# Attention weights of a graph layer as the larger of two exponentials instead of a bent row, a GpSimd addition and one exponential

## The chip, the cores and the metric

One core of a Trainium2 chip. The metric is the time of one execution on the device in microseconds, the median of several runs.

## The reference

Four layers of a graph network over 625 nodes with 256 features and 20000 edges. The change is in layer 1, an attention layer with 4 heads of 64 features:

```python
h = (x @ W).reshape(n, H, F)
a_src = jnp.sum(h * att_src[None], axis=-1)
a_dst = jnp.sum(h * att_dst[None], axis=-1)
e = jax.nn.leaky_relu(a_src[src] + a_dst[dst], 0.2)
m = jax.ops.segment_max(e, dst, num_segments=n)
ex = jnp.exp(e - m[dst])
denom = jax.ops.segment_sum(ex, dst, num_segments=n)
alpha = ex / (denom[dst] + 1e-16)
out = jax.ops.segment_sum(h[src] * alpha[..., None], dst, num_segments=n)
```

The output is 625 x 256 numbers in float32. Layers 0, 2 and 3 and the norms between them are not touched.

## The kernel before, in words

The edges are turned into a dense matrix of counts (`adjT`, sources on the partitions, destinations along the row), in 5 tiles of 125 nodes. Layer 1 then works densely: for each head `h` (4) and each tile `s` of 125 sources (5), so for 20 items `i = 5h + s`, it makes a tile of 125 sources by 625 destinations of attention weights, multiplies it by the counts, and adds its product with the features to that head's sums. All waits between engines are written out by hand with semaphores; each engine runs its own list in order.

- TensorE spreads a column of 625 numbers as a row over all partitions (`spread_row`, five products with the identity). ScalarE copies each spread row out of PSUM (`copy_row`, L520 is its helper). Eight rows stand ahead of the items: `src_row` for 4 heads and `dst_row` for 4 heads.
- VectorE, `best(h, b)`, L1008: the maximum over a destination's sources, one operation for a head and a tile; `down_of(h)`, L1017 to L1021, makes from it the column that brings the row's maximum to zero (`down`). Heads 0 and 1 are done ahead of the items, heads 2 and 3 between them (`AHEAD = 2`). TensorE spreads `down` as one more row per head (`spread_down`), ScalarE copies it over `src_row[h]`.
- An item: ScalarE's `bend`, L629, a Relu of `dst_row` with a bias; GpSimd's addition of `src_row`, L466; ScalarE's `exp`, L636; VectorE's `weigh`, L1027 (`min` with 1, times `adjT`); TensorE's product, the mix, two column ranges into PSUM (it counts up `mixed`). `score` has 7 slots, which a `bend` takes again when the mix of 7 items earlier is done.
- After a head: ScalarE copies its sums (`copy_sums`), TensorE turns them (`turn_sums`, L1406), and VectorE divides and adds the bias (`take_sums`, L1034 to L1043).

ScalarE's list of the stage before:

```python
new_row = {0: 0, 2: 1, 10: 2, 15: 3}
for i in range(HEADS + 2):
    if i < HEADS:
        bend(i)
        if i in new_row:
            copy_row(2 * H + new_row[i])
    if i >= 2:
        exp(i - 2)
    if i >= NT + 3 and i % NT == 3:
        copy_sums(i // NT - 1)
```

Behind the stage come two norms, and then layer 2, whose GpSimd gathers (84 pairs) take the larger part of the kernel; they wait for a table that is stored after these norms.

## Time and profile before

| | us |
|---|---|
| median of 3 runs | 508.77 |
| the runs | 508.77, 507.05, 510.25 |
| the profiled execution, its own time | 509.2 |
| its span | 507.4 |
| busy: TensorE / VectorE / ScalarE / GpSimd | 391.4 / 308.2 / 193.9 / 277.6 |
| the stage of the change: first spread row to the last head's sums | 124.30 to 190.49 |

The busy times are sums over the whole span. The profile names engines PE (TensorE), PEld (TensorE's weight loads), DVE (VectorE), ACT (ScalarE) and POOL (GpSimd). Tiles that share a buffer appear under the buffer's name: `score` is `q_sb`, `arena` or `x`, and `src_row`, `dst_row` and `adjT` are `arena`. PEclk is the granted clock of TensorE as a share of 2.4 GHz.

### The profile page before, as it was taken

Reading aid. Unit: us, or ns where it says so; the run is one execution under the profiler, and the core shown is the slowest. Engines: PE = TensorE matmul, PEld = TensorE weight load, DVE = VectorE, ACT = ScalarE, POOL = GpSimd, SP = SyncE. Lnnn points to the kernel's source line nnn. Section 1 sums busy time; section 2 is a strip of 40 time slices with the busy share of each in tenths; the row PEclk is TensorE's granted clock in tenths of the full one; section 3 lists DMA queues with packets and bytes.
Section 4 is the critical chain, followed back from the end, with each engine's and each line's share of the span. In section 5 each row is a group of like instructions: output and inputs, shape, how many; then the busy total and the mean of one; then the engine's idle time right before and its main releaser. Section 6 shows DMA issues by size and latency. Waiting matters only on the chain.

```text
span 507.4 us, 5439 instructions
## 1 busy us (share of the span) xinstructions
PE 391.4 (77%) x1414; PEld 210.4 (41%) x1415; DVE 308.2 (61%) x596; ACT 193.9 (38%) x497; POOL 277.6 (55%) x278
## 2 busy tenths in 40 slices
PE   2936675799757865897999995799999989889800
PEld 0612222476714432433554542454544444347700
DVE  3479999777699979444444541454455854445243
ACT  1623997314676550253333332243333323212310
POOL 5274875004594540017777777777777777744120
PEclk9878799999857697797999998799999999999965
DMA  5921122000000000036777776777777777720001
GB/s 152 199 83 47 47 70 54 1 1 0 2 1 0 0 1 0 26 105 199 211 210 211 208 213 179 219 209 212 209 210 206 200 213 208 208 59 1 2 3 53
DMA packets 24231, 56.20 MB, mean 111 GB/s; under 512 B 5964, under 2 KB 11279, under 8 KB 24198
## 3 DMA queue, kind: packets, MB, share of 16 engines
q0 software_dynamic: 16224, 48.06, 33.9%
q1 hardware_dynamic: 6800, 6.58, 5.3%
q10 hardware_dynamic: 1174, 1.16, 0.8%
q8 instruction: 16, 0.26, 0.2%
q14 instruction: 17, 0.14, 0.1%
HBM read 53.37 MB, written 2.40 MB: 110 GB/s over the span
## 4 chain that ended last, share of the span: by engine, by line
PE 41%; DVE 19%; POOL 15%; DMA 12%; issue 7%; ACT 4%; ACTq 0%; POOLq 0%; DVEq 0%
PE ps L1198 37%; POOL arena L472 11%; DMA arena<-q_table,t_odd 5%; DVE arena L852 5%; DVE q_sb L1027 3%; DMA hot_table<-x 2%; DMA w_lr<-in_L_gnn_W_r 2%; DVE x L1008 2%; DMA arena<-hot_table,t_even 1%; DVE arena L847 1%; DVE arena L1107 1%; POOL adj L472 1%; DVE stats L920 1%; PE ps L1342 1%; POOL al_g L502 1%
## 5 line engine op out<-in xcount | busy, mean ns | idle before, releaser
L1107 DVE TENSOR_TENSOR arena<-arena,ps 128x1024 f32<-128x1024 f32 x84 | 102.6, 1221 | 111.9 <-DMA arena<-q_table,t_odd 96.1
L1198 PE MATMUL ps<-arena,hot 128*128 128x512 f32 x336 | 165.1, 615 | 0.5 <-DVE arena L1107 0.5
L472 POOL DMA_INDIRECT arena<-q_table,t_even x84 | 79.5, 947 | 68.3 <-DMA q_table<-q_sb 43.1
L472 POOL DMA_INDIRECT arena<-q_table,t_odd x84 | 80.8, 962 | 25.6 <-issue 25.6
L1198 PE MATMUL ps<-parts,hotT 125*128 x168 | 77.5, 543 | 17.1 <-DVE arena L1107 14.2
L1198 PEld LDWEIGHTS ps<-arena,hot 128*128 128x128 f32 x336 | 58.5, 194 | 50.8 <-issue 43.4
L520 ACT ACTIVATE hotT<-ps 125x128 fp32r<-125x128 f32 x84 | 23.3, 277 | 145.9 <-PE ps L1455 145.9
L1198 PEld LDWEIGHTS ps<-parts,hotT 125*128 125x128 f32 x168 | 30.7, 195 | 65.7 <-issue 65.4
L1198 PE MATMUL ps<-arena 128*128 128x376 f16 (+1 forms) x178 | 34.8, 345 | 21.4 <-DVE arena L852 10.8
L852 DVE TENSOR_SCALAR arena<-iota,t_column,t_weight 128x376 f16<-128x376 f16 x140 | 45.3, 396 | 0.0
L434 POOL DMA_INDIRECT arena<-hot_table,t_even x28 | 30.6, 1093 | 13.7 <-issue 6.7
L680 ACT ACTIVATE hot<-h_sb,ones 128x128 fp32r<-128x128 f32 x84 | 32.8, 392 | 0.0
L672 ACT ACTIVATE h_sb<-iota,t_dst 128x128 f32<-128x128 f32 x84 | 32.5, 389 | 0.0
L1198 PE MATMUL ps<-q_sb,h_ones 125*65 125x512 f32 (+1 forms) x48 | 21.8, 596 | 13.8 <-DVE q_sb L1027 13.8
L1198 PEld LDWEIGHTS ps<-arena 128*128 128x128 f16 x178 | 14.8, 104 | 41.3 <-issue 38.2
L466 POOL TENSOR_TENSOR q_sb<-q_sb,arena 125x625 f32<-125x625 f32 x12 | 19.2, 1621 | 18.3 <-ACT q_sb L629 11.5
L563 ACT ACTIVATE x<-iota,t_dst 128x128 f16<-128x128 f16 x84 | 25.9, 388 | 8.1 <-issue 4.8
L1198 PE MATMUL ps<-zeros 128*128 128x512 f16 (+1 forms) x70 | 19.2, 427 | 8.9 <-POOL ident L396 4.2
L1027 DVE SCALAR_TENSOR_TENSOR q_sb<-q_sb,arena 125x625 f32<-125x625 f32 x12 | 19.9, 1674 | 5.8 <-ACT q_sb L636 5.8
L1008 DVE CUSTOM_DVE_ANT_0 x<-arena 125x625 f32<-125x625 f32 x20 | 21.4, 1103 | 2.0 <-ACT arena L520 2.0
L520 ACT ACTIVATE arena<-ps 125x625 f32<-125x625 f32 (+3 forms) x20 | 12.6, 637 | 22.6 <-PE ps L1505 14.9
L520 ACT ACTIVATE xT<-ps 128x500 f32<-128x500 f32 (+2 forms) x13 | 6.9, 553 | 36.6 <-PE ps L1198 18.7
(231 smaller groups left out, 539.0 us busy)
## 6 DMA issues: line engine op xcount, KB each, us to landing
arena<-q_table,t_even POOLq DMA_INDIRECT x84, 3.7
arena<-q_table,t_odd POOLq DMA_INDIRECT x84, 3.7
q_table<-q_sb SPq DMA_DIRECT2D x5, 250.0 KB
w_sb<-in_L_gnn_W SPq DMA_DIRECT2D x1, 1024.0 KB, 12.9
x<-in_x ACTq DMA_DIRECT2D x1, 625.0 KB
out<-x SPq DMA_DIRECT2D x5, 125.0 KB
w_sb<-in_L_gnn_W SPq DMA_DIRECT2D x1, 512.0 KB, 12.2
hot_table<-x SPq DMA_DIRECT2D x1, 459.0 KB
```

The lines of the kernel that those rows point to most:

```text
L434: pool.indirect_dma_start(hot_src[:, j, k, 0, :], None, hot_dram[:, :], bass.IndirectOffsetOnAxis(ap=t_even[:, at:at + 1], axis=0)).then_i ...
L466: nc.gpsimd.tensor_tensor(w, w, src_row[0:NP, h, :], ALU.add).then_inc(leaky, 1)
L472: pool.indirect_dma_start(to, None, q_dram[:, :], bass.IndirectOffsetOnAxis(ap=index, axis=0)).then_inc(done, 16)
L520: return nc.scalar.activation(o, i, ACT.Copy)
L563: last = nc.scalar.activation(apart[:, j, k, :], iota16[:, 0:128], ACT.Abs, bias=t_dst[:, two_item(g, k, 1)], scale=-1.0)
L672: nc.scalar.activation(off_by[:, i % 3, :], iota32[:, :], ACT.Abs, bias=t_dst[:, 2 * i:2 * i + 1], scale=-1.0).then_inc(off_by_done, 1)
L680: nc.scalar.activation(hot[:, i % U, :], off_by[:, i % 3, :], ACT.Relu, bias=ones[:, 0:1], scale=-1.0).then_inc(hot_built, 1)
L852: last = V.tensor_scalar(hot_src[:, j, k, r, :], iota16[:, 0:SHARED], t_column[:, at], t_weight[:, at], ALU.is_equal, ALU.mult)
L1008: step(V.tensor_tensor_reduce(out=spare[len(last_steps) % len(spare)], in0=mask[0:NP, b, 0:N], in1=src_row[0:NP, h, :], scale=1.0, scalar= ...
L1027: V.scalar_tensor_tensor(score[i % SLOTS], score[i % SLOTS], 1.0, adjT[0:NP, s * N:(s + 1) * N], ALU.min, ALU.mult).then_inc(weighted, 1)
L1107: V.tensor_tensor(both, both, ps[:, 5 + i % 2, :].unsqueeze(1).to_broadcast([128, 2, HID]), ALU.max).then_inc(maxed, 1)
L1198: return nc.tensor.matmul(o, a, b, start=start, stop=stop, skip_group_check=True)
```

## The change

With z = a_src + a_dst and m the row's maximum after the leaky relu, exp(max(z, 0.2z) - m) is the larger of exp(z - m) and exp(0.2z - m). Each is one ScalarE pass: an Exp over a spread row with the source's term as bias. So there are two spread rows for each head (`down` = a_dst - m, `down_flat` = 0.2 a_dst - m), both made by `down_of`, and the four rows of `a_dst` are not spread any more. ScalarE's two passes per item are `exp_above` and `exp_below`; VectorE takes the larger of the two in an operation of its own (`join`), one item ahead of `weigh`. The addition on GpSimd and the tile `src4` are gone. `score` is split in 4 slots (`above`, taken again when the mix of 4 items earlier is done) and 3 (`below_zero`, taken again after the join of 3 items earlier). ScalarE copies a head's two rows after the third item of the head before. The two new rows use PSUM where the second bank of turned sums was, so `turn_sums` now has one bank and waits for the sums before to be read.

```diff
@@ -191,6 +191,7 @@
         a3 = a2 + H * N
         top = sb("top", [128, NT, H], f32)
         down = sb("down", [128, NT, H], f32)
+        down_flat = sb("down_flat", [128, NT, H], f32)
         rden = sb("rden", [128, NT, H], f32)
         p0 = U * 2 * HID
         ring = arena[:, 0:p0].rearrange("p (i r f) -> p i r f", i=U, r=2)
@@ -208,13 +209,14 @@
         q_flat = q_sb[:, :, :].rearrange("p b f -> p (b f)")
         score = [q_flat[0:NP, k * N:(k + 1) * N] for k in range(4)] + [arena[0:NP, a3:a3 + N]]
         score += [x0[:, :, :].rearrange("p b f -> p (b f)")[0:NP, k * N:(k + 1) * N] for k in range(2)]
-        SLOTS = len(score)
+        MET = 4
+        above, below_zero = score[0:MET], score[MET:]
+        FLAT_SLOTS = len(below_zero)
 
         prod = [q_sb[:, n, :].rearrange("p (c f) -> p c f", c=DC) for n in range(4)]
         h_ones = sb("h_ones", [128, NT, H, F + 1], f32)
 
         xl, xr = h_ones[:, :, :, :].rearrange("p b h f -> p b (h f)")[:, :, 0:D + 1], x1_bias
-        src4 = sb("src4", [128, NT, H], f32)
         src02 = sb("src02", [128, NT, H], f32)
         hot = sb("hot", [128, U, 128], f32r)
         hotT = sb("hotT", [128, 2, 128], f32r)
@@ -264,7 +266,7 @@
         agg_done, var_ready, std_ready, x_ready = sem("agg_done"), sem("var_ready"), sem("std_ready"), sem("x_ready")
         h_done, h_copied, row_done, row_copied = sem("h_done"), sem("h_copied"), sem("row_done"), sem("row_copied")
         src_scaled, down_ready = sem("src_scaled"), sem("down_ready")
-        bent, leaky, exped, weighted, mixed = sem("bent"), sem("leaky"), sem("exped"), sem("weighted"), sem("mixed")
+        exped, joined, weighted, mixed = sem("exped"), sem("joined"), sem("weighted"), sem("mixed")
         bias_added = sem("bias_added")
         sumT_copied, sum_turned, sum_read = sem("sumT_copied"), sem("sum_turned"), sem("sum_read")
         q_done, q_copied, q_stored = sem("q_done"), sem("q_copied"), sem("q_stored")
@@ -288,7 +290,7 @@
 
         def row_bank(r):
 
-            return 1024 * (r % H) if r < 2 * H else NT * 512
+            return 1024 * r if r < H else NT * 512 + NT * 128 * ((r - H) % 2)
 
         def sT_bank(b):
 
@@ -310,10 +312,6 @@
         def last_turned_out(engine_copy):
 
             return engine_copy(adjT_by[0:NP, NT - 1, (NT - 1) * NP:N], ps[0:NP, 3, 0:NP])
-
-        def sum_bank(h):
-
-            return (4, 7)[h % 2]
 
         def two_item(turn, k, r):
 
@@ -457,14 +455,6 @@
                     for b in range(NT):
                         pool.indirect_dma_start(first_src[0:NP, b:b + 1], None, src.rearrange("(e c) -> e c", c=1),
                                                 bass.IndirectOffsetOnAxis(ap=first_at[0:NP, b:b + 1], axis=0)).then_inc(first_srcs, 16)
-
-                for i in range(HEADS):
-                    h = i // NT
-                    pool.wait_ge(bent, i + 1)
-                    pool.wait_ge(row_copied, 2 * H + h + 1)
-                    w = score[i % SLOTS]
-                    nc.gpsimd.tensor_tensor(w, w, src_row[0:NP, h, :], ALU.add).then_inc(leaky, 1)
-
 
                 pool.wait_ge(q_stored, 16 * (NT + 1))
 
@@ -612,32 +602,32 @@
 
                 def copy_row(r):
 
-                    act.wait_ge(row_done, r + 1)
-                    row = dst_row[0:NP, r - H, :] if H <= r < 2 * H else src_row[0:NP, r % H, :]
+                    act.wait_ge(row_done, r + 1 if r < H else r + 2 - (r - H) % 2)
+                    row = (src_row[0:NP, r, :] if r < H else
+                           (src_row, dst_row)[(r - H) % 2][0:NP, (r - H) // 2, :])
                     at = row_bank(r)
                     copy(row.rearrange("p (b s) -> p b s", b=NT),
                          flat[0:NP, at:at + NT * 128].rearrange("p (b s) -> p b s", b=NT)[:, :, 0:NP]).then_inc(row_copied, 1)
 
-                for r in range(2 * H):
+                for r in range(H):
                     copy_row(r)
 
-                def bend(i):
+                def exp_above(i):
 
                     h, s = i // NT, i % NT
-                    if i >= SLOTS:
-                        act.wait_ge(mixed, i - SLOTS + 1)
-                    nc.scalar.activation(score[i % SLOTS], dst_row[0:NP, h, :], ACT.Relu, bias=src4[0:NP, s, h:h + 1],
-                                         scale=4.0).then_inc(bent, 1)
-
-                def exp(i):
+                    if i >= MET:
+                        act.wait_ge(mixed, i - MET + 1)
+                    nc.scalar.activation(above[i % MET], src_row[0:NP, h, :], ACT.Exp, bias=h_sb[0:NP, s, D + h:D + h + 1])
+
+                def exp_below(i):
 
                     h, s = i // NT, i % NT
-                    act.wait_ge(leaky, i + 1)
-                    nc.scalar.activation(score[i % SLOTS], score[i % SLOTS], ACT.Exp, bias=src02[0:NP, s, h:h + 1],
-                                         scale=0.2).then_inc(exped, 1)
-
-                act.wait_ge(row_copied, 2 * H)
-                act.wait_ge(src_scaled, 2)
+                    if i >= FLAT_SLOTS:
+                        act.wait_ge(joined, i - FLAT_SLOTS + 1)
+                    nc.scalar.activation(below_zero[i % FLAT_SLOTS], dst_row[0:NP, h, :], ACT.Exp,
+                                         bias=src02[0:NP, s, h:h + 1]).then_inc(exped, 1)
+
+                act.wait_ge(src_scaled, 1)
 
                 def copy_sums(h):
 
@@ -646,16 +636,20 @@
                         act.wait_ge(sum_turned, h - 1)
                     copy(xT[0:F + 1, h % 2, :], flat[0:F + 1, 1024 * (h % 2):1024 * (h % 2) + N]).then_inc(sumT_copied, 1)
 
-                new_row = {0: 0, 2: 1, 10: 2, 15: 3}
-                for i in range(HEADS + 2):
-                    if i < HEADS:
-                        bend(i)
-                        if i in new_row:
-                            copy_row(2 * H + new_row[i])
-                    if i >= 2:
-                        exp(i - 2)
-                    if i >= NT + 3 and i % NT == 3:
-                        copy_sums(i // NT - 1)
+                copy_row(H)
+                copy_row(H + 1)
+                act.wait_ge(row_copied, H + 2)
+                for i in range(HEADS):
+                    h, s = i // NT, i % NT
+                    exp_above(i)
+                    exp_below(i)
+                    if s == 2 and h + 1 < H:
+                        copy_row(H + 2 * h + 2)
+                        copy_row(H + 2 * h + 3)
+                    if s == NT - 1 and h + 1 < H:
+                        act.wait_ge(row_copied, H + 2 * h + 4)
+                    if s == 2 and h >= 1:
+                        copy_sums(h - 1)
                 copy_sums(H - 1)
                 root(1)
                 root(2)
@@ -995,7 +989,6 @@
                     at = (b * NT + b) * NP
                     step(V.tensor_tensor(adjT[0:NP, at:at + NP], adjT[0:NP, at:at + NP], ident[0:NP, 0:NP], ALU.add))
                 dve.wait_ge(h_copied, 2 * NT)
-                V.tensor_scalar(src4[0:NP, :, :], h_sb[0:NP, :, D:D + H], 4.0, None, ALU.mult).then_inc(src_scaled, 1)
                 V.tensor_scalar(src02[0:NP, :, :], h_sb[0:NP, :, D:D + H], 0.2, None, ALU.mult).then_inc(src_scaled, 1)
                 last_steps = []
 
@@ -1018,19 +1011,25 @@
                     settle()
                     step(V.scalar_tensor_tensor(top[0:NP, :, h], top[0:NP, :, h], 0.2, top[0:NP, :, h], ALU.mult, ALU.max))
                     settle()
-                    V.scalar_tensor_tensor(down[0:NP, :, h], top[0:NP, :, h], -5.0, a_dst, ALU.mult, ALU.add).then_inc(down_ready, 1)
+                    V.scalar_tensor_tensor(down[0:NP, :, h], top[0:NP, :, h], -1.0, a_dst, ALU.mult, ALU.add).then_inc(down_ready, 1)
+                    V.scalar_tensor_tensor(down_flat[0:NP, :, h], a_dst, 0.2, top[0:NP, :, h], ALU.mult, ALU.subtract).then_inc(down_ready, 1)
+
+                def join(i):
+
+                    dve.wait_ge(exped, i + 1)
+                    V.tensor_tensor(above[i % MET], above[i % MET], below_zero[i % FLAT_SLOTS], ALU.max).then_inc(joined, 1)
 
                 def weigh(i):
 
                     s = i % NT
-                    dve.wait_ge(exped, i + 1)
-                    V.scalar_tensor_tensor(score[i % SLOTS], score[i % SLOTS], 1.0, adjT[0:NP, s * N:(s + 1) * N],
+                    dve.wait_ge(joined, i + 1)
+                    V.scalar_tensor_tensor(above[i % MET], above[i % MET], 1.0, adjT[0:NP, s * N:(s + 1) * N],
                                            ALU.min, ALU.mult).then_inc(weighted, 1)
 
                 def take_sums(h):
 
                     dve.wait_ge(sum_turned, h + 1)
-                    sums = ps[0:NP, sum_bank(h), 0:NT * (F + 1)].rearrange("p (b f) -> p b f", b=NT)
+                    sums = ps[0:NP, 4, 0:NT * (F + 1)].rearrange("p (b f) -> p b f", b=NT)
                     step(V.tensor_scalar(rden[0:NP, :, h], sums[:, :, F], 1e-16, None, ALU.add))
                     settle()
                     step(V.reciprocal(rden[0:NP, :, h], rden[0:NP, :, h]))
@@ -1048,8 +1047,11 @@
                     for b in range(NT):
                         best(h, b)
                     down_of(h)
+                join(0)
                 for h in range(H):
                     for s in range(NT):
+                        if NT * h + s + 1 < HEADS:
+                            join(NT * h + s + 1)
                         weigh(NT * h + s)
                         if h + AHEAD < H:
                             best(h + AHEAD, s)
@@ -1381,29 +1383,26 @@
 
                     for b in range(NT):
                         at = row_bank(r) + 128 * b
-                        last = mm(flat[0:NP, at:at + NP], columns[0:NP, b, r % H:r % H + 1].to_broadcast([NP, NP]),
+                        last = mm(flat[0:NP, at:at + NP], columns[0:NP, b, :].to_broadcast([NP, NP]),
                                   ident[0:NP, 0:NP], True, True)
                     last.then_inc(row_done, 1)
 
                 pe.wait_ge(h_copied, 2 * NT)
                 for r in range(H):
-                    spread_row(r, h_sb[:, :, D:D + H])
-                for r in range(H, 2 * H):
-                    pe.wait_ge(row_copied, r - H + 1)
-                    spread_row(r, h_sb[:, :, D + H:D + 2 * H])
-
+                    spread_row(r, h_sb[:, :, D + r:D + r + 1])
                 def spread_down(h):
-                    pe.wait_ge(down_ready, h + 1)
-                    pe.wait_ge(row_copied, 2 * H + h)
-                    spread_row(2 * H + h, down)
+                    pe.wait_ge(down_ready, 2 * h + 2)
+                    pe.wait_ge(row_copied, H + 2 * h)
+                    spread_row(H + 2 * h, down[0:NP, :, h:h + 1])
+                    spread_row(H + 2 * h + 1, down_flat[0:NP, :, h:h + 1])
 
                 def turn_sums(h):
 
                     pe.wait_ge(sumT_copied, h + 1)
-                    if h >= 2:
-                        pe.wait_ge(sum_read, h - 1)
+                    if h >= 1:
+                        pe.wait_ge(sum_read, h)
                     for b in range(NT):
-                        last = nc.tensor.transpose(ps[0:NP, sum_bank(h), b * (F + 1):(b + 1) * (F + 1)],
+                        last = nc.tensor.transpose(ps[0:NP, 4, b * (F + 1):(b + 1) * (F + 1)],
                                                    xT[0:F + 1, h % 2, b * NP:(b + 1) * NP], ident[0:F + 1, 0:F + 1])
                     last.then_inc(sum_turned, 1)
 
@@ -1420,7 +1419,7 @@
                     pe.wait_ge(weighted, i + 1)
                     for lo, hi in ((0, 512), (512, N)):
                         at = 1024 * (h % 2)
-                        last = mm(flat[0:F + 1, at + lo:at + hi], h_ones[0:NP, s, h, :], score[i % SLOTS][:, lo:hi],
+                        last = mm(flat[0:F + 1, at + lo:at + hi], h_ones[0:NP, s, h, :], above[i % MET][:, lo:hi],
                                   s == 0, s == NT - 1)
                     last.then_inc(mixed, 1)
                 turn_sums(H - 1)
```

## Rows read from the trace of the kernel before

**Rows 1.** Chain of waits, 134 to 192 us: start us, us, engine, tile, line.

```profile
139.33 0.71 ACT q_sb L636
...
145.11 1.82 DVE x L1008
...
146.93 1.81 DVE q_sb L1027
...
152.43 4.44 PE ps L1198 x8
...
190.49 0.18 DVE rden L1034
```

**Rows 2.** Timeline while GpSimd adds rows: start us, us, engine, line, operation.

```profile
142.37 2.08 POOL L466 TENSOR_TENSOR arena<-arena 125x625 f32<-125x625 f32 x1
...
143.00 2.11 DVE L1027 SCALAR_TENSOR_TENSOR q_sb<-q_sb,arena 125x625 f32<-125x625 f32 x1
...
145.03 1.89 DVE L1008 CUSTOM_DVE_ANT_0 x<-arena 125x625 f32<-125x625 f32 x1
```

**Rows 3.** Timeline while GpSimd is idle, VectorE.

```profile
153.75 0.80 DVE L1008 CUSTOM_DVE_ANT_0 x<-arena 125x625 f32<-125x625 f32 x1
...
155.08 0.80 DVE L1027 SCALAR_TENSOR_TENSOR x<-x,arena 125x625 f32<-125x625 f32 x1
...
155.80 0.80 DVE L1008 CUSTOM_DVE_ANT_0 x<-arena 125x625 f32<-125x625 f32 x1
```

**Rows 4.** Groups by shape, 134 to 190 us: count, busy us, mean ns.

```profile
L1027 DVE SCALAR_TENSOR_TENSOR q_sb<-q_sb,arena 125x625 f32<-125x625 f32 x12 | 19.9, 1674 | 5.8 <-ACT q_sb L636 5.8
...
L1008 DVE CUSTOM_DVE_ANT_0 x<-arena 125x625 f32<-125x625 f32 x11 | 14.7, 1340 | 0.0
...
L1027 DVE SCALAR_TENSOR_TENSOR x<-x,arena 125x625 f32<-125x625 f32 x5 | 5.6, 1118 | 1.0 <-ACT x L636 1.0
...
L1027 DVE SCALAR_TENSOR_TENSOR arena<-arena 125x625 f32<-125x625 f32 x3 | 2.4, 800 | 0.0
```

**Rows 5.** Timeline, other VectorE operations.

```profile
130.79 0.17 DVE L1021 SCALAR_TENSOR_TENSOR down<-top,h_sb 125x5 f32<-125x5 f32 x1
...
168.92 0.15 DVE L1034 TENSOR_SCALAR rden<-ps 125x5 f32<-125x5 f32 x1
...
170.39 0.17 DVE L1017 TENSOR_TENSOR top<-top,h_sb 125x5 f32<-125x5 f32 x1
...
198.15 1.49 DVE L1067 TENSOR_TENSOR tmp<-tmp,rows 125x1280 f32<-125x1280 f32 x1
```

**Rows 6.** Timeline, ScalarE: a row's copy, a bend and an exponential.

```profile
138.64 0.69 ACT L520 ACTIVATE arena<-ps 125x625 f32<-125x625 f32 x1 [1.01 <-PE ps L1198]
...
141.34 0.80 ACT L629 ACTIVATE arena<-arena,src 125x625 f32<-125x625 f32 x1
142.05 0.81 ACT L636 ACTIVATE q_sb<-q_sb,src 125x625 f32<-125x625 f32 x1
```

**Rows 7.** Timeline, TensorE: eight rows, one row twice, one mix twice.

```profile
124.30 8.99 PE L1198 MATMUL ps<-ident,h_sb 125*125 125x125 f32 x80 [0.54 <-ACT h_ones L520]
...
134.17 1.32 PE L1198 MATMUL ps<-ident,down 125*125 125x125 f32 x10 [0.87 <-ACT arena L520]
...
136.37 2.23 PE L1198 MATMUL ps<-ident,down 125*125 125x125 f32 x10 [0.87 <-ACT arena L520]
...
160.60 1.27 PE L1198 MATMUL ps<-q_sb,h_ones 125*65 125x512 f32 x4 [0.38 <-DVE q_sb L1027]
...
168.33 2.35 PE L1198 MATMUL ps<-q_sb,h_ones 125*65 125x512 f32 x4 [1.51 <-DVE q_sb L1027]
```

**Rows 8.** Stretches: length, busy of PE, PEld, DVE, ACT, POOL, then granted clock.

```profile
140.00:157.00 17.00, 11.61 (x22) 4.35 (x23) 16.83 (x22) 8.74 (x14) 11.48 (x7) 0.50 0.00 0
...
164.00:174.00 10.00, 7.67 (x19) 4.00 (x20) 9.35 (x16) 4.51 (x7) 5.19 (x3) 0.50 0.00 0
174.00:190.50 16.50, 12.62 (x55) 6.14 (x53) 12.82 (x17) 10.29 (x15) 8.90 (x5) 1.00 0.00 1
```

## The prediction

> **What bounds the kernel now.** I read the chain of waits first, from 134 to 192 us, because the edit touches only the attention of layer 1. Everything in front of 124.30 us, and everything behind the last head's sums at 190.49 us, stays as it is [rows 1]. The reader is to see that the chain alternates between two VectorE lines, L1008 (the maximum over a node's sources) and L1027 (the weights times the adjacency), each holding it for 1.81 to 1.90 us, and now and then crosses to TensorE [rows 1]. Next I read the timeline at two places. While GpSimd adds rows (2.08 us for one), VectorE's two operations last 1.89 and 2.11 us [rows 2]. Where GpSimd has nothing to do, the same two last 0.80 us and start 0.72 to 0.73 us apart [rows 3]. So the bound of the first half of this stage is VectorE made slow by GpSimd. The third view, the groups by shape, sizes that: 20 weighings took 19.9 + 5.6 + 2.4 = 27.9 us where 20 x 0.80 would be 16.0, and 11 maxima took 14.7 where 11 x 0.80 would be 8.8 [rows 4]. The excess is 11.9 + 5.9 = 17.8 us of VectorE's time. Last, the table of stretches: TensorE ran at 1.2 GHz (granted 0.50) from 140 to 157 and from 164 to 174 us and at 2.4 GHz from 174 on [rows 8].
>
> **The change part by part.** *GpSimd's 20 additions go.* With them goes the excess of 17.8 us on VectorE, and the way ScalarE, GpSimd, ScalarE for each score.
>
> *ScalarE does two exponentials in place of a bend and an exponential.* Both kinds of pass over 125x625 last 0.80 to 0.81 us and start 0.71 us apart [rows 6], so a score costs 1.42 us as before. Nothing gained or lost there.
>
> *VectorE gets 20 joins.* The trace shows no maximum of two 625-wide rows. The nearest rows are the two-input operations: the weighing (0.72 us pitch, [rows 3]) and a sum of 1280 elements in 1.49 us [rows 5], which halved is 0.75. I take 0.72. The bounds are 0.80, its whole length, and 0.65, what 625 elements take by the slope between the 625-wide and the 1280-wide operation ((1.49 - 0.80) / 655 elements x 625) (over 20 joins, 1.4 us less to 1.6 us more). They cost 20 x 0.72 = 14.4 us on an engine that is the bound. The added small operation of each head's end is bounded by 0.08 and 0.17 us; I take 0.10. VectorE's balance is thus -17.8 + 14.4 + 0.4, some 3 us to the good: large terms that nearly cancel. The scaling of the source terms by 4 (0.17 us, off the path) goes too.
>
> *Spread rows move.* Before, eight rows are spread ahead of the loop (8.99 us, 1.12 each, [rows 7]) and one per head later. Now four stand ahead, and two per head later, which TensorE can make only when VectorE has that head's maxima. ScalarE queues the two copies behind the third score of the head before; waiting there, it holds every exponential behind them, and VectorE runs out of scores. This is the added wait, and it decides the size.
>
> The path at full clock, in time of the profiled execution:
> 1. The first head's maxima and small operations end at 130.79 + 0.17 + 0.10 = 131.06 [rows 5]. Two rows take 2 x 1.12 + 0.2 = 2.4 us, two copies 1.4, and the second score's last exponential ends four passes later (3 x 0.71 + 0.81 = 2.9). The second join starts at 137.9. TensorE's 4 rows fewer ahead make the start early; before, the first weighing waited for the exponential that the chain ends at 140.04 [rows 1].
> 2. Head 0: five joins, five weighings (10 x 0.72) and five maxima for head 2 (5 x 0.73) are 10.85 us; to 148.7.
> 3. Rows of head 2: maxima's small operations 0.8, two rows 2.4, copies of both and of the sums 3 x 0.69, the next two passes 1.5, handovers 0.1: 6.9 us; to 155.6. VectorE had work for all but some 1.8 us of it.
> 4. Head 1: from there three joins, three weighings and three maxima (6.5 us), then the sums of head 0, whose first and next operations stand 1.47 us apart [rows 5]; to 163.6.
> 5. Rows of head 3: the same 6.9 us, and now VectorE has few operations left to do meanwhile, so it stands about 3.3 us; to 170.5.
> 6. Seven joins, eight weighings (10.8 us), sums of head 1 (1.5), 0.1 of waiting; to 182.9.
> 7. The last mix queues behind the one before it: to the last sums 3.4 us (mix, copy 0.7, turn 0.7, handovers); 186.3.
> Against 190.49 this is 4.2 us earlier.
>
> *The clock.* One spread row lasted 1.32 us at 2.4 GHz and 2.23 us at 1.2 GHz, one mix 1.27 against 2.35 us [rows 7]. A pair of rows at the low clock adds 2.0 us to step 3 or 5. TensorE will be idle before both pairs, and in this stage the clock went down twice, for 17 and for 10 us [rows 8]. Before it came back at 157 us TensorE had been busy for 4.44 us on end [rows 1]. Heads 0 and 1 now offer a mix every 2.17 us, about what one takes at the low clock, so such unbroken work would come sooner, and the low stretches should be shorter. I take one of the two pairs at the low clock: 4.2 - 2.0 = 2.2 us of gain.
>
> VectorE is the bound, and the joins last what every 625-wide operation there lasts, 0.80 us each [rows 3]. The Trainium skill (VectorE: DVE Perf Modes, "Rules for kernel authors") says to keep down the number of VectorE operations, since every one pays for emptying the pipeline; that rule speaks against this change. By it alone the 20 joins would be pure loss; with the rows the loss is 14.4 us, and the excess that goes beside it is 17.8.
>
> **The rivals.** *A: as above*, 2.2 us less. The profiled execution took 509.2 us (its span of 507.4 and 1.8 around it), 0.4 above the median of the runs, so 509.2 - 2.2 = 507.0 there and 508.77 - 2.2 = 506.6 on the median, from which the other cases are counted too. The range of this case is 504.6 (B's value) to 508.6 (both pairs at the low clock, nothing else).
> *B: the clock stays at 2.4 GHz throughout.* For it: from 174 to 190.5 us it stayed high with TensorE busy for 12.62 of 16.5 us [rows 8]. It gives 4.2 us, with cheaper joins (0.65) up to 5.6: 503.2 to 504.6.
> *C: the clock is low from the first head on, slower than before.* Place: steps 3, 5, 6 and 7. Price: 2.0 + 2.0 for the two pairs; from step 6 on TensorE becomes the bound, since a mix at 2.2 us (4.44 for two, [rows 1]) outlasts VectorE's 1.44 us per score, 8 x 0.76 = 6.1; the last mix and turn 1.4. Together 11.5, less 4.2: 7.3 slower, 516.1. It decides against the change from 4.2 us on, that is with both pairs low and any of head 3's mixes too. For it: 27 of the 50 us from 140 on were low before [rows 8]. Against it: at this pace TensorE at 1.2 GHz would be busy without a pause, as it was in front of the rise at 157 us [rows 1]. Halfway (both pairs and half of the mixes) it is 4.0 + 3.0 - 4.2 = 2.8 slower, 511.6.
> The Trainium skill (TensorE: Matmul & The Clock Gate, "HAM oscillation — how this bites in real kernels") describes a kernel whose bursts of products are parted by waits and which starts every burst at half clock; by that this would be rival C.
> *D: the slow VectorE isn't GpSimd's doing*, so the excess stays and the joins come on top, at least 14 us slower: 523. Against it speaks that every 0.80 us operation of [rows 3] stands where GpSimd is idle.
> *E: VectorE's operations speed up, but the exponentials' rings (4 and 3 slots) hold ScalarE back.* At full clock a slot of the first ring comes back after two passes (1.5), two joins and a weighing (2.3), the wait for the next score between them (0.7) and a mix (1.3), 5.8 us, and four scores at 1.44 are 5.8, so it's even; it costs less than 1 us, inside A's range.
> Nothing downstream takes the gain back: what follows waits for the last sums, and GpSimd's next work waits for a table stored after them.
>
> **How the numbers follow.** Chances: A 0.50, B 0.28, C 0.20 (most of it near the halfway point), D 0.02. One per cent is 5.1 us, about what a measurement of this kernel can tell from no change. Faster by over 1% needs more than B's plain 4.2: cheap joins or an unforeseen saving, 0.20. Slower by over 1% needs most of C, or D: 0.08. The rest is 0.72. The range goes from the lower end of B, widened a little because three runs of the same kernel lie 3.2 us apart, to the halfway point of C: 503.2 to 511.6. The predicted time is 506.6.
>
> **What would show it.** In the profile of the changed kernel: L1008's and the weighing's mean at 0.80 us throughout, and joins at 0.75 to 0.80; ScalarE's copies of rows waiting for TensorE for 3 to 5 us at the third score of heads 1 and 2; VectorE's waits on the joins after them of about 2 and 3 us; the last sums starting near 188.3 us in place of 190.49. Wrong would be: the clock low for the whole stage (C), VectorE's mean above 1 us (D), or joins that run faster than 0.65 us. The step that is least sure is the choice of one pair at the low clock.

## The result and the profile after

The changed kernel took 505.96 us in the median of 8 runs (504.41 to 507.86), the kernel before 508.3 us on the same chip (506.69 to 510.38): a ratio of 0.9948, with 0.9926 to 0.997 as its 95% interval. That is 2.6 us less, 1.5 to 3.8.

| | before | after |
|---|---|---|
| profiled execution, its own time, us | 509.2 | 507.86 |
| its span, us | 507.4 | 506.1 |
| first spread row starts, us | 124.30 | 123.48 |
| last head's sums (L1034 before, L1033 after), us | 190.49 | 189.09 |
| from the first to the reciprocal of the second ("the stage"), us | 66.39 | 65.81 |
| VectorE's busy time in the whole span, us | 308.2 | 304.9 |
| GpSimd's | 277.6 | 243.9 |

The reciprocal is one step behind the row of the last sums, 190.69 and 189.29 us; the stage's length is counted to it in all that follows. The two profiled executions are 1.3 us apart, and only 0.6 us of that lie in the stage; 0.8 us lie in front of it, where the first spread row starts.

In the kernel after, `weigh` is L1026, `join` L1020, `best` L1001, `exp_above` L620, `exp_below` L627, a row's copy L510. First the groups by shape, 134 to 190 us, columns as in [rows 4]:

```profile
L1026 DVE SCALAR_TENSOR_TENSOR q_sb<-q_sb,arena 125x625 f32<-125x625 f32 x20 | 16.0, 804 | 0.0
L1020 DVE TENSOR_TENSOR q_sb<-q_sb,x 125x625 f32<-125x625 f32 x13 | 10.5, 807 | 7.1 <-ACT x L627 7.1
L1001 DVE CUSTOM_DVE_ANT_0 x<-arena 125x625 f32<-125x625 f32 x10 | 8.1, 806 | 0.0
L1020 DVE TENSOR_TENSOR q_sb<-q_sb,arena 125x625 f32<-125x625 f32 x7 | 5.6, 807 | 2.8 <-ACT arena L627 2.8
```

These answer to [rows 4]: the weighings fell from 27.9 to 16.0 us, and a maximum from 1340 to 806 ns. The joins added 16.1 us of busy time. Large terms that nearly cancel, as forecast, and behind them, in the last column of the joins, 9.9 us in which VectorE had nothing to do but wait for ScalarE; the weighings of [rows 4] have 6.8 us of such waits.

Where these waits stand is in the timeline of the kernel after:

```profile
131.45 2.30 PE L1200 MATMUL ps<-ident,down_flat 125*125 125x125 f32 x10
...
135.27 2.44 PE L1200 MATMUL ps<-ident,down 125*125 125x125 f32 x10 [1.52 <-ACT arena L510]
...
138.12 0.81 DVE L1020 TENSOR_TENSOR q_sb<-q_sb,x 125x625 f32<-125x625 f32 x1 [0.60 <-ACT x L627]
...
153.56 1.27 ACT L510 ACTIVATE arena<-ps 125x625 f32<-125x625 f32 x2 [4.50 <-PE ps L1200]
...
156.84 0.81 DVE L1020 TENSOR_TENSOR q_sb<-q_sb,x 125x625 f32<-125x625 f32 x1 [2.75 <-ACT x L627]
...
168.02 1.28 ACT L510 ACTIVATE arena<-ps 125x625 f32<-125x625 f32 x2 [3.53 <-PE ps L1200]
...
171.30 0.81 DVE L1020 TENSOR_TENSOR q_sb<-q_sb,x 125x625 f32<-125x625 f32 x1 [2.94 <-ACT x L627]
...
178.32 0.82 ACT L620 ACTIVATE q_sb<-arena,h_sb 125x625 f32<-125x625 f32 x1 [1.53 <-PE ps L1200]
...
179.88 0.81 DVE L1020 TENSOR_TENSOR q_sb<-q_sb,x 125x625 f32<-125x625 f32 x1 [0.76 <-ACT x L627]
...
189.09 0.17 DVE L1033 TENSOR_SCALAR rden<-ps 125x5 f32<-125x5 f32 x1 [2.01 <-PE ps L1405]
```

Read the brackets: ScalarE stood 4.50 and 3.53 us before it could copy the rows of heads 2 and 3, and VectorE then stood 2.75 and 2.94 us before the ninth and the fourteenth join. This is the wait that the change adds. The first two rows show head 0's second and head 1's first spread row made at the low clock, 2.30 and 2.44 us, where [rows 7] have 1.32 us for the high one. The rows at 178.32 and 179.88 us show a second way: ScalarE waits 1.53 us for a mix, whose slot its exponential takes again, and VectorE then waits 0.76 us for that exponential.

A stretch of the chain of waits in the kernel after, behind the fourteenth join (columns as in [rows 1]):

```profile
171.30 0.81 DVE q_sb L1020
172.11 0.73 DVE q_sb L1026
172.84 0.04 issue
172.89 2.35 PE ps L1200 x4
175.23 0.97 PE ps L1405 x5
176.20 3.69 PE ps L1200 x8
179.89 0.02 issue
179.91 0.69 ACT xT L510
```

Here the chain lies on TensorE for 7.0 of 8.6 us: mixes at 2.35 us, which is the low clock's price in [rows 7].

### The profile page after: what moved, and what is told of

Its sections match the earlier page's. It is cut to its first block, busy times and chain, and to the rows that moved or that the text cites. A ratio compares the mean times of both kernels' runs of the same rounds, so it can differ in the third digit from the quotient of the medians.

```text
span 506.1 us, 5426 instructions
## 1 busy us (share of the span) xinstructions
PE 392.7 (78%) x1414; PEld 209.9 (41%) x1415; DVE 304.9 (60%) x619; ACT 193.9 (38%) x497; POOL 243.9 (48%) x258
## 4 chain that ended last, share of the span: by engine, by line
PE 36%; DVE 25%; POOL 16%; DMA 8%; issue 7%; ACT 4%; SPq 2%; DVEq 0%; ACTq 0%; POOLq 0%
PE ps L1200 33%; POOL arena L462 13%; DVE arena L846 9%; DMA arena<-q_table,t_odd 5%; DMA g<-in_L_gnn_weight 3%; DVE arena L841 2%; DVE x L1001 2%; DVE q_sb L1026 1%; DVE q_sb L1020 1%; DVE arena L1109 1%; POOL adj L462 1%; DVE stats L914 1%; ACT arena L510 1%; POOL al_g L492 1%; ACT xT L510 1%
## 5 line engine op out<-in xcount | busy, mean ns | idle before, releaser
L1200 PE MATMUL ps<-parts,hotT 125*128 x168 | 75.4, 531 | 15.5 <-DVE arena L1109 11.7
L510 ACT ACTIVATE hotT<-ps 125x128 fp32r<-125x128 f32 x84 | 23.3, 278 | 145.8 <-PE ps L1454 145.8
L1200 PE MATMUL ps<-arena 128*128 128x376 f16 (+1 forms) x178 | 33.4, 330 | 21.4 <-DVE arena L846 12.3
L1200 PE MATMUL ps<-q_sb,h_ones 125*65 125x512 f32 (+1 forms) x80 | 28.8, 502 | 11.2 <-DVE q_sb L1026 11.2
L1200 PEld LDWEIGHTS ps<-arena 128*128 128x128 f16 x178 | 13.1, 100 | 41.5 <-issue 39.1
L510 ACT ACTIVATE arena<-ps 125x625 f32<-125x625 f32 (+3 forms) x20 | 12.2, 635 | 31.7 <-PE ps L1200 15.7
L1200 PEld LDWEIGHTS ps<-q_sb,h_ones 125*65 125x65 f32 x80 | 11.0, 157 | 28.0 <-issue 14.9
L1454 PE MATMUL ps<-ident_r,hot 128*128 128x128 f32 x84 | 19.2, 228 | 1.5 <-issue 1.5
L620 ACT ACTIVATE q_sb<-arena,h_sb 125x625 f32<-125x625 f32 x20 | 16.2, 810 | 5.7 <-PE ps L1200 5.6
L1200 PE MATMUL ps<-w_lrT,xT 128*125 128x512 f32 x20 | 12.8, 785 | 7.0 <-DVE words L822 6.8
```

What stands on the lines that cost most here:

```text
L510: return nc.scalar.activation(o, i, ACT.Copy)
L620: nc.scalar.activation(above[i % MET], src_row[0:NP, h, :], ACT.Exp, bias=h_sb[0:NP, s, D + h:D + h + 1])
L1200: return nc.tensor.matmul(o, a, b, start=start, stop=stop, skip_group_check=True)
L1454: nc.tensor.transpose(ps[:, 7, 0:128].bitcast(f32r), hot[:, i % U, :], ident_r[:, :]).then_inc(hot_turned, 1)
```

## Experiments

Four kernels ran on one chip, four on a second, four on a third, each set beside the kernel before. The first set ran on a chip on which the kernel before took 541.57 us, 33 us more than elsewhere (why is in the last section), so its runs are compared by their difference from that, and by the length of the stage.

| run | median, us | kernel before there | ratio, 95% interval | stage, us | granted clock in it |
|---|---|---|---|---|---|
| before, first profile | 508.77 | | | 66.39 | 0.77 |
| changed, first comparison | 505.96 | 508.3 | 0.9948 (0.9926 to 0.997) | 65.81 | 0.84 |
| no additions | 521.38 | 541.57 | 0.9615 (0.9589 to 0.9641) | 48.27 | 0.96 |
| no joins | 529.11 | 541.57 | 0.978 (0.9733 to 0.9828) | 51.80 | 0.93 |
| joins on GpSimd | 546.09 | 541.57 | 1.0083 (1.0043 to 1.0124) | 71.77 | 0.81 |
| late copies | 535.61 | 541.57 | 0.9892 (0.9858 to 0.9925) | 61.03 | 0.89 |
| changed, again | 503.51 | 507.4 | 0.9919 (0.9889 to 0.9948) | 61.38 | 0.92 |
| zero products | 504.78 | 507.4 | 0.9927 (0.9899 to 0.9955) | 63.21 | 1.00 |
| late copies and zero products | 503.4 | 507.4 | 0.9896 (0.9868 to 0.9925) | 60.81 | 1.00 |
| fills on GpSimd | 503.84 | 507.4 | 0.9928 (0.9895 to 0.9961) | 64.11 | 0.84 |
| changed, third time | 501.33 | 507.95 | 0.9882 (0.9844 to 0.992) | 65.14 | 0.87 |
| late copies, again | 501.52 | 507.95 | 0.9874 (0.9847 to 0.9901) | 62.81 | 0.89 |
| late copies, early column | 501.53 | 507.95 | 0.9866 (0.9826 to 0.9907) | 60.79 | 0.92 |
| the same with zero products | 499.98 | 507.95 | 0.9853 (0.9826 to 0.988) | 58.24 | 1.00 |

The stage is that of each kernel's one profiled execution; the medians are over 3 to 10 runs.

**1. The kernel before without GpSimd's additions.**

```diff
-                for i in range(HEADS):
-                    ...
-                    nc.gpsimd.tensor_tensor(w, w, src_row[0:NP, h, :], ALU.add).then_inc(leaky, 1)
...
                 def exp(i):
...
-                    act.wait_ge(leaky, i + 1)
+                    act.wait_ge(bent, i + 1)
```

> The kernel before, with GpSimd's 20 additions left out: the exponential waits for its bend alone and src_row is not added, so the weights are others. Theory 1 (GpSimd's additions made VectorE slow, 17.8 us of excess, and stood in each score's way): every weighing and maximum lasts 0.80 us, ScalarE's 1.42 us per score becomes the pace, the last sums come 15 to 17 us earlier, 491 to 494 us. Theory 2 (the 1.8 us operations have another cause): they stay at 1.8 us where they were, only the way through GpSimd goes, 2 to 5 us less, 503 to 506 us.

Measured: 20.2 us less than the kernel before on its chip, and a stage of 48.27 us in place of 66.39, 18.1 less; both are somewhat more than the 15 to 17 us expected. VectorE's busy time in the stage fell from 53.9 to 35.9 us, by 18.0. Its groups by line:

```profile
L1002 DVE CUSTOM_DVE_ANT_0 x<-arena 125x625 f32<-125x625 f32 x20 | 15.6, 807 | 2.0 <-ACT arena L514 2.0
L1021 DVE SCALAR_TENSOR_TENSOR q_sb<-q_sb,arena 125x625 f32<-125x625 f32 x12 | 9.6, 808 | 5.8 <-ACT q_sb L630 5.8
```

The same weighings that took 1674 ns in [rows 4] take 808 ns. Nothing but GpSimd's work was taken away, so the 1.8 us operations were its doing; theory 2 falls.

**2. The changed kernel without joins.** `join` and its calls go, `weigh` waits for `exped`, and `exp_below` waits for `weighted`.

> The changed kernel with the 20 joins left out: the weighing takes the first exponential alone, so the weights are others. Theory 1 (VectorE is the bound except where it waits for rows, so each join costs its 0.72 us): 15 of the 20 lie on the path, heads 0 and 1 go at ScalarE's 1.42 us per score, 9 us less than the changed kernel, about 497 us. Rival (the waits for the spread rows and TensorE's clock set the stage, the joins fill time in which VectorE would wait anyway): less than 3 us less, 503 us or more.

Measured: 12.5 us less than the kernel before. The late copies (experiment 5), which ran beside it, took 6.0 less with the joins in place, so 6.5 us more than this kernel. The stage took 51.80 us; the changed kernel's stage at a similar granted clock (0.92) took 61.38, so 20 joins cost 9.6 us on the path, 0.48 each of the 0.72 that VectorE spends on one. This is one profile of each, from two chips, and rough: the four times of this kernel lie 7.1 us apart (524.38 to 531.48), the profiled one is the fastest, and it made its first pair of rows at the low clock, which cost it 0.9 us. The rival of filled waits falls by the medians too.

**3. The joins on GpSimd.** VectorE's calls of `join` go, and GpSimd adds the two rows.

```diff
+                for i in range(HEADS):
+                    pool.wait_ge(exped, i + 1)
+                    nc.gpsimd.tensor_tensor(above[i % MET], above[i % MET], below_zero[i % FLAT_SLOTS], ALU.add).then_inc(joined, 1)
```

> The changed kernel with the joins on GpSimd, as additions of the same two rows in place of the maximum, so the weights are others. Theory 1 (any GpSimd operation that reads rows makes VectorE's two-input operations slow): they last 1.8 to 2.1 us again, 3.6 us per score in heads 0 and 1, and the time is 511 to 516 us, at or above the kernel before. Theory 2 (the slowness of before lay elsewhere): they stay at 0.80 us, VectorE loses 14.4 us of work, 495 to 499 us.

Measured: 4.5 us more than the kernel before, in the forecast band, with a stage of 71.77 us. Its timeline:

```profile
138.89 2.07 POOL L461 TENSOR_TENSOR q_sb<-q_sb,x 125x625 f32<-125x625 f32 x1
139.53 2.10 DVE L1030 SCALAR_TENSOR_TENSOR q_sb<-q_sb,arena 125x625 f32<-125x625 f32 x1
...
141.55 1.90 DVE L1005 CUSTOM_DVE_ANT_0 x<-arena 125x625 f32<-125x625 f32 x1
...
147.44 0.80 DVE L1030 SCALAR_TENSOR_TENSOR q_sb<-q_sb,arena 125x625 f32<-125x625 f32 x1
```

With GpSimd back on the rows, VectorE's operations last 1.90 and 2.10 us again, and 0.80 as soon as it pauses. VectorE is busy for 53.3 us of the stage, as in the kernel before (53.9), and waits longer. So two exponentials and a maximum are of no use by themselves: the change pays because the maximum is on VectorE.

**4. GpSimd fills a row that nobody reads.** In the changed kernel, 20 fills of 125x625, one for each score:

```diff
+                for i in range(HEADS):
+                    pool.wait_ge(exped, i + 1)
+                    ...
+                    nc.gpsimd.memset(scratch[0:NP, :], 0.0).then_inc(cleared, 1)
```

> The changed kernel, in which GpSimd fills an unused row of 625 with zeros 20 times, once for each score, while VectorE works: it writes and reads nothing. Theory 1 in its narrow form (a two-input operation of VectorE is held up only by GpSimd's reading): VectorE's operations stay at 0.80 us and the time within 1 us of the changed kernel. Wide form (any GpSimd operation on these rows holds VectorE up): they last over 1.0 us while a fill runs, 5 us or more above the changed kernel.

Its groups by line:

```profile
L1034 DVE SCALAR_TENSOR_TENSOR q_sb<-q_sb,arena 125x625 f32<-125x625 f32 x20 | 16.0, 803 | 0.0
...
L465 POOL MEMSET scratch<- 125x625 f32 x20 | 12.4, 621 | 40.1 <-ACT x L635 25.0 <-ACT arena L635 15.1
```

Two rows of its timeline:

```profile
141.78 0.81 DVE L1034 SCALAR_TENSOR_TENSOR q_sb<-q_sb,arena 125x625 f32<-125x625 f32 x1
...
142.13 0.62 POOL L465 MEMSET scratch<- 125x625 f32 x1 [0.80 <-ACT x L635]
```

20 fills of 621 ns beside VectorE's work, and a weighing still lasts 803 ns; the time is 0.3 us above the changed kernel beside it. The narrow form holds. The Trainium skill (SBUF — State Buffer, "Who interferes with whom") says that a VectorE instruction with two inputs in SBUF contends with a GpSimd instruction that reads SBUF and not with one that only writes; the additions and this run agree with it, at 1.9 to 2.1 us and 0.80 us.

**5. The copies of the rows behind the fifth score.**

```diff
-                    if s == 2 and h + 1 < H:
+                    if s == 2 and h >= 1:
+                        copy_sums(h - 1)
+                    if s == NT - 1 and h + 1 < H:
                         copy_row(H + 2 * h + 2)
                         copy_row(H + 2 * h + 3)
-                    if s == NT - 1 and h + 1 < H:
                         act.wait_ge(row_copied, H + 2 * h + 4)
-                    if s == 2 and h >= 1:
-                        copy_sums(h - 1)
```

> The changed kernel, with ScalarE's two copies of a head's rows behind the fifth score of the head before instead of the third; nothing else differs. Theory 1 (in the changed kernel the copies wait for TensorE's rows and hold back the two scores queued behind them, 2.75 and 2.94 us of VectorE's idle time): those two waits shrink to 1 us or less, 2 to 3.5 us less than the changed kernel, about 503 us. Rival (the rows themselves come too late, whatever is queued behind them): the waits only move to the next head's first score, within 1 us of the changed kernel, 505 to 507 us.

> Late copies (behind the fifth score) on the same chip as the changed kernel. The wait of 1.48 us at the ninth join goes, that of 2.94 us at the fourteenth becomes two of about 1.2. Theory 1 (what stands in ScalarE's queue decides): 1.5 to 3 us less than the changed kernel beside it. Rival (TensorE's clock decides, and differs from run to run): within 1 us of it.

The changed kernel without an edit ran beside the second:

> The changed kernel unaltered once more, as the measure for the three runs beside it: 2.5 to 4 us less than the kernel before.

Two joins of the run with late copies (first), and the waits that they stand for in the changed kernel, run again (second):

```profile
166.74 0.81 DVE L1019 TENSOR_TENSOR q_sb<-q_sb,x 125x625 f32<-125x625 f32 x1 [0.83 <-ACT x L627]
...
169.45 0.81 DVE L1019 TENSOR_TENSOR q_sb<-q_sb,arena 125x625 f32<-125x625 f32 x1 [1.18 <-ACT arena L627]
```

```profile
154.53 0.81 DVE L1020 TENSOR_TENSOR q_sb<-q_sb,x 125x625 f32<-125x625 f32 x1 [1.48 <-ACT x L627]
...
168.99 0.81 DVE L1020 TENSOR_TENSOR q_sb<-q_sb,x 125x625 f32<-125x625 f32 x1 [2.94 <-ACT x L627]
```

The wait of 1.48 us is gone and that of 2.94 is parted into three (0.83, 1.18 and 1.18 us), so what stood in ScalarE's queue did make them. But on one chip the two kernels took 501.52 and 501.33 us: no difference. The profiled stages were 61.03 against 61.38, and 62.81 against 65.14 us. I had expected 1.5 to 3 us; by the medians the rival holds. (The changed kernel itself was 6.6 us faster than the kernel before, where 2.5 to 4 were expected.) The changed kernel's six times there (500.05, 500.2, 501.19, 501.47, 505.55, 505.67) lie 5.6 us apart, those with late copies 1.1 (500.62 to 501.69). The profiled execution of the changed kernel is the one of 505.55 us, and it has the first pair of rows and the mixes behind the fourteenth join at the low clock: a stage of 65.14 us is not its median. In the second profile with late copies, too, the first pair of rows fell into the low clock: the first join waited 2.78 us, in the first profile of that kernel 1.13. Both have a mean clock of 0.89, and their stages are 62.81 and 61.03 us.

**6. Products of zeros that keep TensorE busy.**

```diff
+                def warm(products, h):
+                    at = 1024 * (h % 2) + 640
+                    for k in range(products):
+                        mm(flat[:, at:at + 384], zeros[:, 0:128], zeros[:, 0:384], True, True)
+                pe.wait_ge(row_copied, 1)
+                warm(12, 0)
...
                 spread_down(0)
+                warm(8, 0)
...
                     last.then_inc(mixed, 1)
+                    if s < NT - 1:
+                        warm(4, h)
```

The 12 products stand ahead of the first pair of rows. Each of these products begins a sum (the first `True`) in a bank in which the mixes gather their columns 512 to 624, and this kernel's output is off by a relative 0.077; most likely the mixes' sums begin anew with them, which was not tried by itself. The instructions and their order are otherwise those of the changed kernel.

> The changed kernel unaltered, as the measure for the runs beside it. Theory 1: 2 to 3.5 us less than the kernel before, as in the first comparison. Rival (its gain belongs to the one chip on which it was measured first): no difference.

> The changed kernel with products of zeros that nobody reads on TensorE: 12 ahead of the first pair of rows, 8 behind it, 4 after every mix but a head's last. Theory 1 (the low clock took what the sum at full clock promised, 3.4 us in the profiled execution): TensorE's clock stays at 2.4 GHz for most of the stage, which takes 61.5 to 63.5 us, 1.5 to 3 us less than the changed kernel beside it. Rival (the rows' way through ScalarE and VectorE sets the stage, at either clock): the clock rises, the time doesn't move by 1 us. Second rival (the added products stand in front of mixes and rows): slower than the changed kernel by 1 us or more.

The stage as one stretch, of the changed kernel in the first comparison, of its second run, and with the zero products (columns as in [rows 8]):

```profile
123.48:189.29 65.81, 48.41 (x220) 30.56 (x220) 50.55 (x110) 40.31 (x57) 5.28 (x4) 0.84 0.02 1
```

```profile
123.47:184.85 61.38, 44.97 (x220) 27.62 (x220) 50.37 (x110) 40.30 (x57) 5.29 (x4) 0.92 0.02 1
```

```profile
122.85:186.06 63.21, 53.33 (x304) 33.03 (x304) 50.48 (x111) 40.32 (x57) 5.28 (x4) 1.00 0.02 1
```

The clock did stay at 2.4 GHz, but the time was 1.3 us above the changed kernel beside it. That kernel beside it was 3.9 us faster than the kernel before, somewhat more than the 2 to 3.5 expected, and not on the first chip: the rival of one chip's gain falls. Its stage, at 0.92, had lost nothing to the clock up to the fourteenth join, which came 45.52 us behind the first row in both: one low stretch lay over head 1's second row, the other over the mixes of head 1, where a mix of 2.35 us fits VectorE's pace:

```profile
156.11 2.35 PE L1200 MATMUL ps<-q_sb,h_ones 125*65 125x512 f32 x4 [2.47 <-DVE q_sb L1026]
...
168.99 0.81 DVE L1020 TENSOR_TENSOR q_sb<-q_sb,x 125x625 f32<-125x625 f32 x1 [2.94 <-ACT x L627]
...
170.57 1.27 PE L1200 MATMUL ps<-q_sb,h_ones 125*65 125x512 f32 x4 [2.80 <-DVE q_sb L1026]
```

And the zero products stood in front of the last mixes: 4.3 us from the reciprocal of head 2 to that of head 3, against 3.3 us; another 0.8 us was lost between the fourteenth join and the reciprocal of head 2. So the second rival came in at the end of the stage, and the first part of theory 1 (the clock took 3.4 us of the first profile) is borne out only by comparing executions of the same kernel, 65.81 and 65.14 against 61.38 us.

**7. Late copies with the zero products, and head 3's column ahead of the sums of head 0.** The first is runs 5 and 6 together. The second puts `down_of(h + AHEAD)` ahead of `take_sums(h - 1)` in VectorE's list. In the third the zero products add to unread columns and begin no sum (`False, True`), and head 3 has none.

> Both alterations: the copies of a head's rows behind the fifth score, and the products of zeros. Theory 1 (two separate losses): the stage takes 58.8 to 60 us against 61.0 with late copies alone, 5 to 6.5 us less than the changed kernel beside it, about 8.5 us less than the kernel before. Rival (both remove the same wait): no more than the larger of the two, 3 to 5 us less than the changed kernel.

> Late copies, and VectorE makes head 3's column ahead of the sums of head 0 instead of behind them, so that TensorE can spread its rows 1.47 us earlier. Theory 1 (the path to head 3 runs through VectorE's queue): the waits at the fourteenth and sixteenth join shrink from 2.4 us together to 1 or less, 1 to 1.5 us less than late copies alone, 3.5 to 5 us less than the changed kernel. Rival (ScalarE, which has 37 us of passes and copies for 20 scores, becomes the bound of the last two heads): less than 0.5 us less than late copies alone.

> As the run before, with products of zeros on TensorE: 12 ahead of the first pair of rows, 8 behind it and 4 after each mix of heads 0 to 2 but a head's last; here they add to columns that nobody reads and begin no sum. Theory 1: a granted clock of 1.0 for all of the stage but its end, and no product of zeros in front of the last mixes, so 0 to 1.5 us less than the run before, and less spread between executions. Rival: the products cost what the clock gives, no difference or up to 1 us more.

The first gave 60.81 us of stage, missing the forecast of 58.8 to 60, and the same median as the changed kernel (503.4 and 503.51), where both theory and rival had it at least 3 us faster. Its tail had the same 4.3 us. The second missed too: 501.53 against 501.52 for late copies alone. Its waits in heads 2 and 3 shrank to 1.18 and 0.86 us, not to 1 together, and its first pair of rows fell into the low clock. The third shows what the two give without that:

```profile
122.28:180.52 58.24, 51.12 (x288) 31.48 (x288) 50.37 (x110) 40.85 (x57) 5.28 (x4) 1.00 0.02 1
```

```profile
134.48 0.81 DVE L1019 TENSOR_TENSOR q_sb<-q_sb,arena 125x625 f32<-125x625 f32 x1 [1.13 <-ACT arena L627]
...
135.90 0.81 DVE L1019 TENSOR_TENSOR q_sb<-q_sb,x 125x625 f32<-125x625 f32 x1 [0.60 <-ACT x L627]
...
167.54 0.81 DVE L1019 TENSOR_TENSOR q_sb<-q_sb,arena 125x625 f32<-125x625 f32 x1 [1.18 <-ACT arena L627]
```

These are all of its joins' waits, 2.9 us where the changed kernel had 9.9 in its first profile and 6.2 in its second. It is the fastest of all kernels here, 499.98 us (499.08 to 500.96), 0.9853 of the kernel before. Against the second it is 1.55 us less, at the edge of the forecast, and its five times lie 1.9 us apart where the second's six lie 6.1, as forecast. Against the changed kernel beside it that is 1.35 us in the median, and the two intervals overlap; that it beats the changed kernel is likely and not shown.

## Why the prediction was right

The forecast was 506.6 us and 2.2 us of gain; measured were 505.96 us and 2.6 us. The mechanism came as described, but that the numbers lie so near each other is in part luck: the gain at full clock was put too low and the loss to the clock too low as well (both below), and in the profiled executions the stage gave 0.6 us and not 2.2. The last sums stood at 189.09 us where 188.3 was forecast, 1.4 us earlier than before, and 0.8 of that stems from the first row's earlier start. Step by step, in time from the first spread row:

| | forecast, full clock | zero products (clock 1.00) | changed, again (0.92) | changed, first (0.84) |
|---|---|---|---|---|
| second join starts | 13.6 | 13.61 | 13.61 | 14.64 |
| head 2's column begins | 24.4 | 24.58 | 24.59 | 25.62 |
| ninth join | 31.3 | 31.06 | 31.06 | 33.36 |
| head 3's column begins | 39.3 | 39.05 | 39.04 | 41.35 |
| fourteenth join | 46.2 | 45.52 | 45.52 | 47.82 |
| last reciprocal | 62.2 | 63.21 | 61.38 | 65.81 |

- *The excess of 17.8 us goes with the additions*: right. Experiment 1 took 18.0 us out of VectorE's busy time and 18.1 us out of the stage.
- *20 joins at 0.72*: right in the pitch (0.72 in the chain, 0.80 long). On the path they cost 9.6 us, since VectorE waits part of the time.
- *Spread rows move, and ScalarE's copies hold the exponentials back*: right in place and nearly in size. The two waits at full clock are 1.48 and 2.94 us, foretold as 1.8 and 3.3; each of steps 3 and 5 takes 6.5 us and not 6.9, in part since ScalarE's copies start 0.58 us apart and not 0.69.
- *The balance, from runs*: 66.39 us, less 18.1 without additions (48.27), plus 3.5 for the second row of each head and what goes with it (51.80), plus 9.6 for joins (61.38). The middle step is the difference of two kernels at clocks of 0.96 and 0.93.
- *The clock*: this was the term that was mis-sized. I took one pair of rows at the low clock, 2.0 us. The first profile lost 1.0 us in the first pair, 1.3 between there and the ninth join, none at head 3's rows and 2.1 in the mixes behind the fourteenth join, 4.4 in all against the second run's stage. The place was wrong too: I had put the 2.0 us at step 3 or 5, and half of the loss came behind both, where I had allowed for it in C alone. The second run lost nothing that shows. The record of the kernel before was also read too kindly: its row of 2.23 us at 136.37 [rows 7] was already at the low clock (granted 0.64 from 136 to 138 us, 0.50 from 138 on), so the first low stretch was some 20 us long and not 17. The clock is thus not a fixed price of this kernel but what makes its executions differ.
- *B's size*: at full clock I forecast 4.2 us of gain; the second run's stage, which lost nothing to the clock, is 5.0 us shorter than before. The three comparisons gave 2.6, 4.1 and 6.0 us (by their ratios, of 508). The last is more than the sum at full clock can explain, and as a ratio it is below the forecast's lower end, as is its median of 501.33 us. Part may be that [rows 1 to 8] are of one execution of the kernel before: its stage lay at a clock of 0.77, and its first row came at 124.30 us, where the changed kernel's three stand at 122.6 to 123.5 (all kernels with the change: 122.06 to 124.98). Nothing in the edit touches that part. This was not tried and stays open.
- Rival C (low clock throughout) didn't come, but a part of its step 6 did: mixes of 2.35 us behind the fourteenth join. D falls by experiments 1 and 3.
- E, the rings, cost nothing at full clock: the second run has no wait of VectorE behind the fourteenth join but the last sums'. At the low clock they are one of the ways by which the slow mixes reached VectorE. ScalarE waited 1.18 and 1.53 us for mixes before it could take their slots again, and VectorE's waits there (0.53 us for the turned sums, 0.76 us before the eighteenth join, behind the second of those waits, and 0.63 us before the nineteenth, behind a copy of sums that had to wait for the same mixes) make up 1.9 of the 2.1 us. The sum for E was made at full clock only.

## What to carry to other kernels

A busy engine's mean duration should be read in stretches with and without its neighbour: 0.80 against 1.9 us for the same instruction said that moving 20 operations onto the bound engine could still win. When an engine's list holds a copy that waits for a far chain, look at what stands behind it; but a wait that is taken away gives time only if the rest of the path is shorter: here a wait of 1.48 us went, the median stood still, and the waits behind the first two joins still came to 3.2 us where 4.4 had been. A margin that was worked out at full clock, like that of the slots here, has to be worked out at the low clock too. Where a low clock falls matters, and not only how long it lasts: the kernel with late copies took 61.03 and 62.81 us of stage at the same mean clock of 0.89, and the changed kernel's low stretches at 0.92 cost it nothing that shows.

## What the runs showed of the hardware

The kernel before took 541.57 us on one chip and 507.4 to 508.3 on three others, and nearly all of the difference lies in layer 2's gathers. VectorE's maxima there, in the kernel with late copies on that chip, and in the same kernel on another:

```profile
L1108 DVE TENSOR_TENSOR arena<-arena,ps 128x1024 f32<-128x1024 f32 x84 | 102.5, 1221 | 143.7 <-remote 66.0
```

```profile
L1108 DVE TENSOR_TENSOR arena<-arena,ps 128x1024 f32<-128x1024 f32 x84 | 102.5, 1221 | 111.7 <-DMA arena<-q_table,t_odd 99.7
```

The operations are equal to the nanosecond; the idle time in front of them is 32 us longer. From the first gather to the last maximum it was 254.2 against 223.3 us, 30.9 of the 33.1 us by which the two spans differ. The stage of the change took 61.03 us on the slow chip and 62.81 on the other, so it was not slower there. That the gathers' transfers are what was slower is likely and not shown: on the slow chip the profile puts 66.0 of the 143.7 us down to another core or an unknown queue (`remote`). Late copies gave 6.0 us over the kernel before on the one chip and 6.4 on the other: a difference in us can be carried over between such chips.
